# A macaron layer on eight cores: weight conversion pieces queued after every seventh attention step, where it was every fifth

## The reference

```python
x = L0_attn_hidden_states
x = x + 0.5 * _L0_ffn_ref(_layernorm(x, axis=-1), L0_ffn_A, L0_ffn_B, L0_ffn_Wr, L0_ffn_br)
x = x + _L0_attn_ref(_layernorm(x, axis=-1), L0_attn_Wq, L0_attn_Wo, L0_attn_kv_cache, L0_attn_block_table)
x = x + 0.5 * _L0_ffn_ref(_layernorm(x, axis=-1), L0_ffn_A, L0_ffn_B, L0_ffn_Wr, L0_ffn_br)
...
def _L0_attn_ref(hidden_states, Wq, Wo, kv_cache, block_table):
    q = (hidden_states @ Wq).reshape(B, S, NUM_HEADS, HEAD_DIM).transpose(0, 2, 1, 3)
    q = _rope(q)
    ...
    scores = jnp.einsum('bhsd,bhtd->bhst', q, K) / jnp.sqrt(jnp.float32(HEAD_DIM))
    attn = jax.nn.softmax(scores, axis=-1)
    ctx = jnp.einsum('bhst,bhtd->bhsd', attn, V)
    ctx = ctx.transpose(0, 2, 1, 3).reshape(B, S, H)
    return ctx @ Wo
```

## Time and profile before

| | us |
|---|---|
| two runs, slowest core | 5327.53 and 5598.6 (median 5463.06) |
| the profiled execution's own time | 5333.38 |
| its span on core 2, the slowest | 5331.8 |
| spans of the other cores | 5294.8 to 5330.2 |
| PE busy | 4065.8 (76%) |
| ACT busy | 2343.5 (44%) |
| POOL busy | 858.8 (16%) |
| DVE busy | 679.9 (13%) |

### The profile page before, as it was taken

The page is one execution under the profiler, slowest core; times in us unless marked ns, Lnnn a source line. Parts: engine busy times, 40 slices in busy tenths (PEclk is TensorE's granted clock), DMA queues, the critical chain, the costliest instruction groups (busy, mean ns, idle before and its releaser), DMA issues.

```text
span 5331.8 us, 46811 instructions; the slowest of 8 cores (5294.8 to 5331.8 us)
## 1 busy us (share of the span) xinstructions
PE 4065.8 (76%) x16880; PEld 1695.2 (32%) x17224; DVE 679.9 (13%) x937; ACT 2343.5 (44%) x2193; POOL 858.8 (16%) x850
## 2 busy tenths in 40 slices
PE   2556678968779778798801354899999999999885
PEld 0122233423334333343300011334444444444331
DVE  2531110000000000000000454320000000000015
ACT  0000047757658567580000000018888888888000
POOL 4531111111111111110012356000000000000004
PEclk9678889989889889899955555999999999999995
DMA  3168875564665656647743402431122202220432
GB/s 76 16 58 78 78 91 79 82 87 70 91 85 75 90 75 85 90 77 173 178 71 53 138 12 43 137 101 17 16 32 32 32 1 32 32 32 1 134 119 71
DMA packets 660859, 378.58 MB, mean 71 GB/s; under 512 B 553120, under 2 KB 553120, under 8 KB 660640
## 3 DMA queue, kind: packets, MB, share of 16 engines
q0 software_dynamic: 553440, 174.22, 31.6%
q10 hardware_dynamic: 51680, 99.63, 5.9%
q1 hardware_dynamic: 55520, 101.74, 5.3%
HBM read 465.83 MB, written 83.89 MB: 103 GB/s over the span
## 4 chain that ended last, share of the span: by engine, by line
DMA 46%; PE 35%; POOL 8%; issue 7%; ACT 2%; DVE 1%; SPq 1%; another core or an unknown queue 0%; POOLq 0%; ACTq 0%; DVEq 0%
DMA PCB<-wo 13%; DMA PCB<-wq 12%; PE pc L553 8%; PE pl L541 7%; DMA wob<-PCB 7%; DMA wqb<-PCB 6%; PE psA L424 6%; DMA WB<-wq 4%; PE psB L513 4%; PE psA L513 4%; POOL SQr L202 4%; PE psA L619 3%; POOL XN L260 2%; DMA WB<-wob 2%; PE pl L217 2%
## 5 line engine op out<-in xcount | busy, mean ns | idle before, releaser
L520 ACT ACTIVATE PS<-psA,CST 128x1024 bf16<-128x1024 f32 x1024 | 1139.3, 1113 | 1239.8 <-PE psA L513 1228.8
L541 PE MATMUL pl<-PS,ONES 128*128 128x512 bf16 x4013 | 1536.7, 383 | 4.5 <-issue 0.2
L553 PE MATMUL pc<-PS,VT 128*128 128x512 bf16 x4013 | 1534.9, 382 | 5.7 <-DMA VT<-vt 1.3
L520 ACT ACTIVATE PS<-psB,CST 128x1024 bf16<-128x1024 f32 x1024 | 1138.8, 1112 | 185.9 <-PE psB L513 181.6
L513 PE MATMUL psA<-QC,KT 128*128 128x512 bf16 x2008 | 613.4, 386 | 284.0 <-DMA KT<-kt 266.2
L424 PE MATMUL psA<-XN,WB 128*128 128x512 bf16 x2008 | 531.0, 422 | 239.9 <-DMA WB<-wq 154.4
L513 PE MATMUL psB<-QC,KT 128*128 128x512 bf16 x2008 | 614.0, 386 | 20.6 <-ACT PS L520 13.2
L541 PEld LDWEIGHTS pl<-PS,ONES 128*128 128x128 bf16 x4096 | 404.4, 99 | 495.7 <-issue 21.7
L553 PEld LDWEIGHTS pc<-PS,VT 128*128 128x128 bf16 x4096 | 404.0, 99 | 496.6 <-issue 21.8
L238 ACT ACTIVATE G<-RSD,CST 128x512 f32<-128x512 f32 x6 | 4.3, 722 | 1202.4 <-DVE RSD L232 1202.4
L619 PE MATMUL psA<-QC,WB 128*128 128x512 bf16 x2006 | 458.4, 382 | 78.3 <-DMA WB<-wob 71.8
(11 more groups left out here) (57 smaller groups left out, 1499.1 us busy)
## 6 DMA issues: line engine op xcount, KB each, us to landing
WB<-wob ACTq DMA_DIRECT2D x128, 512.0 KB, 4.0
WB<-wq POOLq DMA_DIRECT2D x66, 512.0 KB, 7.6
KT<-kt POOLq DMA_DIRECT2D x64, 512.0 KB, 6.7
VT<-vt POOLq DMA_DIRECT2D x64, 512.0 KB, 9.8
PCB<-wo POOLq DMA_DIRECT2D x128, 256.0 KB, 4.6
wob<-PCB SPq DMA_DIRECT2D x128, 256.0 KB, 2.0
PCB<-wq POOLq DMA_DIRECT2D x128, 256.0 KB, 4.7
wqb<-PCB SPq DMA_DIRECT2D x128, 256.0 KB, 2.1
```

The source lines that it names most:

```text
L520: (lambda slot=slot, big=big: lambda sc: sc.activation(PS4[:, slot * CH:(slot + 2) * CH], big[:, :], AF.Exp, bias=CST[:, 0:1], scale=ISQ))(),
L541: (lambda lb=lb, slot=slot, t=t, j=j: lambda tt: tt.matmul(BNK[lb], ONES[:, :], PS4[:, (slot + t) * CH:(slot + t + 1) * CH], start=(j == 0 ...
L553: (lambda g=g, j=j, slot=slot, t=t, cb=cb: lambda tt: tt.matmul(BNK[cb], VT[:, j * 128:(j + 1) * 128], PS4[:, (slot + t) * CH:(slot + t + ...
```

## The change

One number changes: a piece of the weight conversion is queued at flushes whose counter is a multiple of 7, where it was a multiple of 5. The number of pieces, their order among themselves, their size and all waits stay.

```diff
@@ -559,7 +559,7 @@
                         free[("kvslab", j // SLAB)] = (sPE, pe_ctx)
                         if g + 1 < NG:
                             emit_kv_slab(c, g + 1, j // SLAB, ktv, vtv)
-                if flushctr[0] % 5 == 0:
+                if flushctr[0] % 7 == 0:
                     precast_pump(1)
                 flushctr[0] += 1
                 if grp == NK // 2 - 1:
```

## The result

| | kernel before | changed kernel |
|---|---|---|
| all runs, median us | 5509.51 (10 runs) | 5425.28 (11 runs) |
| lowest us | 5327.13 | 5392.94 |
| ratio, 95% interval | 1 | 1.014 [1.0113, 1.0167] |

The changed kernel is 1.4% slower, and the interval leaves no doubt of the sign. By the 2% bound this counts as no change.

What follows compares the result with a forecast made beforehand. The serial chain of 256 pumps through one buffer was taken as the bound; the first square behind it comes 56 us later, the rest unchanged: 5333.4 + 56 = 5389.4 us (+1.1%), range 5350 to 5430.

Steps and rivals of the forecast that it cites:

- the chain and not the attention is the bound: From 756 to 2888 us, 256 serial pumps (load, write-out through single buffer PCB) set the time; attention and WO lie beside.
- POOL waits for PE with every seventh flush: First attention, per group of four heads: POOL needs 160 us, PE 170.7 us, so POOL waits 11 us.
- rival 1: POOL stays the limit, nothing moves, if a slab (pair of KT loads) costs 7.7 us or more: 5315 to 5333 us; chance 0.06.
- PE sets the pace at 1363 us: First attention should take the second attention's 1363 us, ending at 2096 instead of 2390, 294 us earlier.
- Last slab load 1930, WO over 2381, first square 2945, the rest 2443: Forecast timeline in us: last KT load, end of WO, first layer-norm square behind the pumps, then unchanged length to the end.
- Pumps: 7.61 beside attention, 9.50 beside WO, 7.245 alone: Price in us of one weight-conversion piece on POOL's queue in each stretch, read from the trace.
- the clock would hold in the dense attention: First attention without PE's waits would be granted 0.99 of the clock, as the second attention is, instead of 0.92.
- The rival that was priced beside the peak-current rule: Lower clock in the dense first attention, 0.81 instead of 0.99: last slab 265 us later, 5654 us; chance 0.02.
- Seven groups x 11 us = 77 us of waiting: First attention: POOL's added waits for PE; less 18 us saved by 49 pumps running alone, 59 us later.
- The other way to the 56 us: First layer-norm square behind the pumps, timed step by step: 2945 against 2889 us, 56 us later.
- 2 (the gain arrives): PE's gain of 294 us in the first attention reaches the end: 5039 us; chance 0.01.
- 4 (pumps alone dearer): Pumps running alone behind WO cost 9.50 us each instead of 7.245: 173 us more, 5562 us; chance 0.05.

Runs made afterwards that it cites:

- e2: A piece every sixth flush where the kernel before has every fifth; 5324.1 us (one time).
- e4: A piece every fourth flush where the kernel before has every fifth; 5401.1 us (one time).
- e1: The changed kernel (every seventh flush) run again without edit, for its profile; 5383.0 us.
- e5: The kernel before (every fifth flush) run again without edit, for its profile; 5302.7 us.
- e6: The changed kernel (every seventh flush) again, on the chip and in the session of e5; 5382.4, 5383.0 and 5422.2 us, ratio 1.0173.
- e7: The changed kernel with the last 77 pieces queued behind the feed-forward that follows WO; 5377.7 to 5394.2 us, ratio 1.0169 to the kernel before.
- e3: A piece every eighth flush where the kernel before has every fifth; 5498.0 to 5516.8 us, ratio 1.0399.
- e8: The kernel before (every fifth flush) with two PCB buffers used in turn instead of one; 4860.0 to 4910.0 us, ratio 0.9202.
- e9: Two PCB buffers as in e8, but a piece every seventh flush instead of every fifth; 5017.5 and 5020.5 us.

## Why the prediction was wrong, and where it was right

The recorded figure, 5389.4 us, is 1.3% below the median of 5463.06 that was listed for the kernel before; beside that number it stands for a gain. The kernel got slower by 1.4%. The text had set the figure beside the profiled execution's 5333.4, which makes it +1.1% (1.05 before rounding), and the mechanism behind it held; but even so it lies just outside the measured interval of +1.13% to +1.67%.

Step by step:

- **That the chain and not the attention is the bound:** right. e2 gains 226 us of attention and no end; e4 ends the pumps earlier and loses.
- **That POOL waits for PE with every seventh flush:** right. The 28 intervals with a slab in them take 16.2 us on average in e1 (core 7) instead of 12.9 before on that core, 28 x 3.3 = 93 us of waiting; the second sum had 77. In the bounds, POOL's spare time over four slabs is 170.7 - 139.2 = 31.5 us and not 30.9, so rival 1 begins at 7.9 us per slab and not at 7.7; nothing else changes by it.
- **That PE sets the pace at 1363 us:** 1359 to 1366 on the eight cores of e1.
- **Last slab load 1930, WO over 2381, first square 2945, the rest 2443:** 1933, 2392, 2938, 2443.
- **Pumps: 7.61 beside attention, 9.50 beside WO, 7.245 alone:** in e1 on core 7 they take 7.42, 9.12 and 7.31 (120, 32 and 74 intervals, the long one of 13.9 us at the end of WO among the last).
- **That the clock would hold in the dense attention:** right for the times compared here, 0.99 in e1. The rival that was priced beside the peak-current rule of the Trainium skill (TensorE: Matmul & The Clock Gate, Part 1) did not come true in them. But in the first profile of the changed kernel (5670 us) cores 2 and 3 had 0.82 granted through the first attention, which took 1625 us there, while cores 0 and 1 of the same die had 0.99 and took 1359 and 1362: "the trace does not agree" was more than one profile could say.

**The step that failed** is the size of a term, not the mechanism: "Seven groups x 11 us = 77 us of waiting". That is the wait of POOL for PE which the change adds to the chain, and it measured 97 us. The table has the means over the eight cores of e5 and e6. It takes the intervals between the issues of the pumps on POOL's timeline, from the second pump to the last:

| | e5, every fifth | e6, every seventh | difference | forecast |
|---|---|---|---|---|
| the 28 intervals with a slab's loads in them, us | 346.2 | 442.8 | +96.6 | +77 |
| the other 226 intervals, us | 1742.8 | 1728.5 | -14.3 | -18 |
| last pump issued at, us | 2840 | 2920 | +80 | +59 |

The rest is the start of the chain, which is 2 us earlier in e6. The first session shows the same on cores 0 and 1 of the changed kernel's first profile, which had 0.99 granted through the first attention. Core 0 there, from 735 to 2080 us, columns as in rows 3:

```profile
735.00:2080.00 1345.00, 1325.19 (x6097) 594.42 (x6095) 21.48 (x32) 1154.74 (x1079) 178.01 (x205) 1.00 0.58 81
```

The last pump on POOL's timeline of core 0, in that profile:

```profile
2923.20 0.88 POOL L460 DMA_DIRECT2D PCB<-wq  x1 [6.39 <-DMA wqb<-PCB]
```

and in the profile of the kernel before:

```profile
2853.58 0.87 POOL L460 DMA_DIRECT2D PCB<-wq  x1 [6.21 <-DMA wqb<-PCB]
```

The last pump comes 69.6 us later on core 0 and 68.3 us later on core 1, with 82.6 and 98.3 us more in the 28 intervals.

The 11 us per group came out too small because a plain pump was priced at 7.61 us, from 18 intervals on core 2, whose chain ended last in that execution. Ahead of the last slab load the mean of all eight cores is 7.53 us in that profile, 7.49 in e5 and 7.48 in e6, and a slab adds 4.9 us in e5. With these a group costs POOL 18.3 x 7.48 + 4 x 4.9 = 156.5 us, it waits 14 us, and seven groups make 99 us. This is an estimate made afterwards, beside the 96.6 measured.

The other way to the 56 us, "2945, against 2889", has the same fault in another form. The new end was right to 7 us on the slowest core of e1 and to 5 on that of e6. The old end was core 2's, the latest of eight: the mean of the cores is 2864 in that profile and 2840 in e5, and e5's slowest core has its first square at 2861. Every pump of the old chain carries its price into its end, while those ahead of the last slab in the new one are absorbed by PE's pace, so a base read from a core with dear pumps gives too late an old end and too small a difference.

The same may explain why the difference is not the same in every session. Both kernels were longer in the first one. The mean span of the eight cores is 5313 us in the first profile of the kernel before and 5283 in e5; it is 5376 to 5388 us in the compared executions of the changed kernel in the first session and 5363 and 5365 in the profiled ones of e1 and e6. On cores 0 and 1 the 226 intervals take 27 and 24 us more in the first session's profile of the changed kernel than in e1, some 0.1 us per pump. In the old chain 256 pumps carry such a rise into the end, in the new one the 128 behind the last slab; that this makes the old kernel move more, by 30 us against some 18, is argued, not shown by a run of its own, and why a pump cost more there stays open.

The range, 5350 to 5430, holds the times that were compared (5392.94 to 5425.28). Rivals 1 (POOL stays the limit), 2 (the gain arrives) and 4 (pumps alone dearer) fell: POOL waited, the wait at the squares grew to 546 us, and a pump alone took 7.31.

## What to carry to other kernels

Find the queue that holds a serial chain of transfers and cost that chain end to end: a step that spreads its pieces costs nothing while the queue is never made to wait, and each wait added ahead of the leftover pieces comes out at the end, less what those pieces save by running alone (97 us of waiting gave 80). Follow each half of a moved transfer to its own queue (e7 lost its whole gain on the queue of the write-outs). And where the chain turns around in one buffer, a second buffer was worth more here than any place tried for the pieces: with it 5300 us became 4860, and 4800 with every fourth flush.

## What was not expected

- One program takes a different time in different sessions: the kernel before 5327 to 5333 us in the first and 5287 to 5310 in the others, the changed kernel 5393 to 5425 in the first and 5382 to 5422 later.
- A plain pump beside the first attention does not cost the same on every core. Ahead of the last slab load it took 7.31 to 7.58 us by core in e1; the mean of the eight cores is 7.53 in the profile before, 7.46 in e1, 7.38 in e3 and 7.39 in e4. No run separates the cause.
- Pumps beside WO make it longer. WO took 251 us without them, 285 with some 31 (e1), 315 with 40 (e8) and 349 with 61 (e9): 1.1 us per pump with one buffer, 1.6 with two. The fastest version is the one whose pumps all end inside the attention.
